# Moving the second half of group 2 and all of group 3 from VectorE to GpSimd in the step back from the FP6 grid

## What is computed

```python
h = _layernorm(x) * (1 + cb) + sb            # cb, sb, gb: per batch
blocks = h.reshape(rows, K // 32, 32)
scales = max(max(abs(blocks)) / 7.5, eps)    # one per block of 32
xq = nearest_on_fp6_grid(blocks / scales)    # "to the grid"
xd = xq * scales                             # "from the grid"
out = xd @ wd.T + bias                       # 512 x 512 weights
x = x + gb * out
```

## Time and profile before

| what | us |
|---|---|
| median of 3 runs | 339.31 |
| lowest and highest | 336.63, 339.8 |
| profiled execution | 338.35 |
| span of its instructions | 336.3 |
| TensorE busy | 304.5 |
| VectorE busy | 290.4 |
| ScalarE busy | 239.9 |
| GpSimd busy | 227.5 |

### The profile page before, as it was taken

How to read it: one execution, slowest core, us unless ns; L and a number is a source line. 1 busy time by engine, 2 the same in 40 slices (tenths; PEclk the granted TensorE clock), 3 DMA queues, 4 the chain that set the end, 5 groups by cost and what they waited for, 6 DMA issues and landing times. The chain is left out here.

```text
span 336.3 us, 6060 instructions
## 1 busy us (share of the span) xinstructions
PE 304.5 (91%) x2159; PEld 227.8 (68%) x2159; DVE 290.4 (86%) x512; ACT 239.9 (71%) x536; POOL 227.5 (68%) x122
## 2 busy tenths in 40 slices
PE   7879999785899989998999999996999998998993
PEld 5213547565798777786888678874787785776782
DVE  4678759979999799799989979999798899989753
ACT  3278845698679979799998989976799875322410
POOL 1449393599748886969999996977878967722100
PEclk9999998979699999999999999999799999999999
DMA  6999699999979839996899699964773693303133
GB/s 185 394 406 399 231 150 239 355 307 346 225 174 241 154 134 225 276 212 232 136 236 271 221 229 247 248 175 79 228 117 127 185 146 142 127 0 125 49 140 94
DMA packets 23971, 69.00 MB, mean 205 GB/s; under 512 B 2387, under 2 KB 2516, under 8 KB 19974
## 3 DMA queue, kind: packets, MB, share of 16 engines
q1 hardware_dynamic: 16304, 53.83, 48.0%
q0 software_dynamic: 7392, 14.68, 26.0%
q10 hardware_dynamic: 246, 0.12, 0.2%
HBM read 51.48 MB, written 17.14 MB: 204 GB/s over the span
## 5 line engine op out<-in xcount | busy, mean ns | idle before, releaser
L746 PE MATMUL ps<-WH,XH 128*128 128x512 f32 x256 | 108.8, 427 | 1.1 <-issue 0.9
L746 PE MATMUL ps<-WL,XH 128*128 128x512 f32 x256 | 103.3, 405 | 0.0
L379 POOL TENSOR_TENSOR U<-U,c_bc 128x1024 f32<-128x1024 f32 x31 | 74.6, 2408 | 39.0 <-ACT U L474 38.4
L390 POOL TENSOR_TENSOR U<-U,sb_bc 128x1024 f32<-128x1024 f32 x31 | 74.4, 2399 | 2.5
L746 PE MATMUL ps<-WH,XL 128*128 128x512 f32 x256 | 69.7, 394 | 0.2 <-DVE XL L1196 0.2
L463 ACT COPY ps<-bias_bc 128x512 f32<-128x512 f32 x61 | 36.0, 590 | 38.9 <-DVE X L1261 38.9
L1255 DVE TENSOR_TENSOR ps<-ps,gb_bc 128x512 f32<-128x512 f32 x64 | 44.3, 692 | 15.7 <-PE ps L746 15.6
L746 PEld LDWEIGHTS ps<-WH,XH 128*128 128x128 f32 x256 | 50.0, 195 | 11.0 <-ACT XH L454 2.0
L746 PEld LDWEIGHTS ps<-WL,XH 128*128 128x128 f32 x256 | 50.2, 196 | 10.2 <-issue 1.1
L746 PEld LDWEIGHTS ps<-WH,XL 128*128 128x128 f32 x256 | 48.9, 191 | 11.8 <-DVE XL L1196 0.7
L454 ACT ACTIVATE XH<-ps 128x512 fp32r<-128x512 f32 x64 | 37.5, 587 | 22.8 <-PE ps L724 22.7
(11 more groups left out here) (212 smaller groups left out, 351.1 us busy)
## 6 DMA issues: line engine op xcount, KB each, us to landing
X<-in_x SPq DMA_DIRECT2D x16, 1024.0 KB, 8.6
out<-X SPq DMA_DIRECT2D x15, 1024.0 KB, 4.7
X<-mod_scratch POOLq DMA_DIRECT2D x14, 1024.0 KB, 10.9
X<-in_wmod SPq DMA_DIRECT2D x2, 1024.0 KB, 12.3
sb_bc<-mod_scratch SPq DMA_DIRECT2D x7, 256.0 KB, 8.0
c_bc<-mod_scratch SPq DMA_DIRECT2D x7, 256.0 KB, 6.6
gb_bc<-mod_scratch SPq DMA_DIRECT2D x7, 256.0 KB, 8.2
msp<-mod_scratch SPq DMA_DIRECT2D x8, 160.0 KB, 9.8
```

Source lines behind the costliest of these rows:

```text
L379: nc.gpsimd.tensor_tensor(a, a, spread(c_bc[:, b % 2, :]), ALU.mult).then_inc(u_done, 2 if g == 0 else 1)
L390: nc.gpsimd.tensor_tensor(a, a, spread(sb_bc[:, b % 2, :]), ALU.add).then_inc(h_done, 2 if g == 0 else 1)
L746: return M(bank, a[:, k * P:(k + 1) * P], w[:, k, :], start=False, stop=last, skip_group_check=n >= 3)
```

## The change

The border between the engines moves from a whole group to a half. BY_VECTOR = 5 halves stay with VectorE, counted 2g+h: both halves of groups 0 and 1, and the first half of group 2. The halves (2, 1), (3, 0) and (3, 1) go to GpSimd, at the places in its list where later groups have them. VectorE copies the scales to s32 half by half for these three; from group 4 on still a group at a time. to_grid no longer waits for the copy's signal s32_done; GpSimd's from_grid does. Because GpSimd now reads Q8 for these halves, to_grid(3, 1) and to_grid(4, h) wait for xd1_done.

```diff
+        BY_VECTOR = 2 * 2 + 1
@@ GpSimd
             def from_grid(g, h):
                 pool.wait_ge(xt_done, TILES * (g - 2) + HALF * (h + 1))
+                pool.wait_ge(s32_done, 2 * g + h + 1 - BY_VECTOR)
                 pool.wait_ge(q_done, 2 * g + h + 1)
...
-                if g - 1 > FILLING:
+                if 2 * (g - 1) >= BY_VECTOR:
                     from_grid(g - 1, 0)
                 plus_sb(g, 1)
-                if g - 1 > FILLING:
+                if 2 * (g - 1) + 1 >= BY_VECTOR:
                     from_grid(g - 1, 1)
@@ TensorE, transposes
-                if g <= FILLING:
-                    pe.wait_ge(xd_done, 2 * g + j // HALF + 1)
+                half = 2 * g + j // HALF
+                if half < BY_VECTOR:
+                    pe.wait_ge(xd_done, half + 1)
                 else:
-                    pe.wait_ge(xd1_done, 2 * (g - FILLING - 1) + j // HALF + 1)
+                    pe.wait_ge(xd1_done, half - BY_VECTOR + 1)
@@ VectorE, block_scales
-                if g > FILLING:
-                    if g - 2 > FILLING:
-                        dve.wait_ge(xd1_done, 2 * (g - 2 - FILLING))
-                    W_.tensor_copy(s32[:, g % 2, :, :], s64).then_inc(s32_done, 1)
+                if 2 * g + h0 >= BY_VECTOR:
+                    if 2 * (g - 2) + h1 > BY_VECTOR:
+                        dve.wait_ge(xd1_done, 2 * (g - 2) + h1 - BY_VECTOR)
+                    W_.tensor_copy(s32[:, g % 2, h0:h1, :], s64[:, h0:h1, :]).then_inc(s32_done, h1 - h0)
@@ VectorE, to_grid
-                if g > FILLING:
-                    dve.wait_ge(s32_done, g - FILLING)
-                    if g - 1 > FILLING:
-                        dve.wait_ge(xd1_done, 2 * (g - 2 - FILLING) + h + 1)
+                if 2 * (g - 1) + h >= BY_VECTOR:
+                    dve.wait_ge(xd1_done, 2 * (g - 1) + h + 1 - BY_VECTOR)
@@ VectorE, slots THIRD and SECOND
-                    from_grid(g, 1)
+                    if 2 * g + 1 < BY_VECTOR:
+                        from_grid(g, 1)
...
-                    from_grid(g, 0)
+                    if 2 * g < BY_VECTOR:
+                        from_grid(g, 0)
```

## The result

| | before | changed |
|---|---|---|
| median, us (10 runs each) | 338.79 | 335.45 |
| lowest and highest | 336.63, 339.83 | 333.47, 336.71 |
| profiled execution | 338.35 | 336.71 |
| its span | 336.3 | 334.9 |

The ratio is 0.9907 (95% interval 0.9887 to 0.9927): the change makes the kernel 0.9% or some 3.2 us faster. I had forecast 339.0 us with a range of 336.3 to 341.5, and 0.3 us of effect. That was wrong. In experiments 5, 9, 10 and 12 one or two single runs are over 1.5% slower than the fastest of their kernel: the medians given count them, the ratios and intervals leave them out, and the traces of experiments 5 and 9 are of such runs.

The account below looks back on a forecast made before the run. It took the path as VectorE's half (2, 0) until 85 us, TensorE until 106.8, ScalarE until 118, then TensorE; 338.35 - 0 - 0.3 = 338.05, on the median 339.31 - 0.3 = 339.0 us, range 336.3 to 341.5.

Parts of the forecast that it names:

- Value on the path: 0: Before 107 us: net 3.0 us taken off VectorE brings 0, bounds 0 and 3.7 us.
- The replay of GpSimd's list: 92 to 111 us: three added multiplications, 5.75 us, fit; delay taken in by GpSimd's idle 3.74 us before 128.98.
- the two transfers: Groups 6 and 7: issued 5.3 and 3.8 us later, landing before ScalarE's reads at 110.37 and, at median, 124.02.
- there the whole gain has turned into a longer wait: At 112.82 us VectorE, relieved earlier, waits for ScalarE; that wait was to be 1.4 us or longer.
- Rival A: VectorE leads from 85 to 110 us: 333.9 us at most, 336.3 with the first part alone; chance 0.05.
- Rival B: At 226 us L1134 escapes its collision with GpSimd's multiplication: 1.9 us less, 337.1 us; chance 0.08.
- The wait that to_grid loses: All 12 later groups: to_grid starts 0.1 to 0.2 us earlier each; bounds 0 to 2.4 us, 0.3 taken.
- in the chain that ended last there is one such place: At 212.31 us, the one place on that chain where VectorE leads and to_grid's earlier start counts: 0.2 us.
- The rule on two SBUF inputs: 92 to 111 us: relocated GpSimd work slows only VectorE instructions with two SBUF inputs; none in the three windows checked.

Follow-up runs that it names:

- experiment 5: Changed kernel with the one-column comparison near 226 us written as an operation with a scalar instead of two tensors: 333.04 us, ratio to before 0.9827.
- experiment 9: Changed kernel with the scalar form of experiment 5 and the head's five row casts and differences moved to VectorE's slot 1: 327.82 us, ratio to before 0.9672.
- experiment 10: Kernel of experiment 9 with the border as before the change (BY_VECTOR = 8, VectorE takes all of groups 2 and 3): 330.03 us, ratio to before 0.9734.
- experiment 12: The kernel of experiment 10 run once more, unchanged: 330.22 us, ratio to before 0.9724.
- experiment 2: Changed kernel with only the halves moved: GpSimd's wait for s32_done taken out, VectorE's put back: 338.58 us, ratio to before 1.0001.
- experiment 1: Changed kernel with the border put back (BY_VECTOR = 8), so only the waits are exchanged: 335.96 us, ratio to before 0.9920.
- experiment 4: Changed kernel without GpSimd's s32_done wait for the second half of every group from 4 on: 337.98 us, ratio to before 0.9973.
- experiment 6: Changed kernel with the head's five row casts and differences moved from VectorE's slots 5 and 6 to slot 7: 343.11 us, ratio to before 1.0133.

## Why the prediction was wrong

**The move itself: right.** "Value on the path: 0" is experiment 2, 1.0001. The replay of GpSimd's list came within 0.5 us at all three multiplications and the two transfers stayed in time. That the relief turns into waiting for ScalarE was right, the place wasn't: "there the whole gain has turned into a longer wait" names 112.82, where it should have been 102 and 106 us, and the wait at 113 us is 1.56 us in experiment 1 too, where nothing was relieved. Rival A, which came nearest to the measured time, was right in the number and wrong in the cause: with A, experiment 2 would have gained 3 us. Rival B didn't come: in the changed kernel the comparison of one column starts at 225.44, 0.26 us into GpSimd's multiplication, and still takes 2.14 us.

**The wait that to_grid loses: right in kind, too small.** The term was 0.3 us, with the one place of the chain at 212 us. By the trace of experiment 4 it is 0.4 to 0.6 us, and 0.9 by its ratio (0.1 to 1.7 by the interval). The mistake is in "in the chain that ended last there is one such place": that chain began only at 212.2 us and listed 9% of the span for VectorE; a stretch that it doesn't show isn't a stretch where VectorE never leads. The additions come 0.17 us earlier at tiles 15, 19, 35, 39, 43, 47 and 51, and 0.52 us at tile 23, much of which is given back one or two tiles later.

**The wait that GpSimd gets: the step that failed.** The prediction counts s32_done as a wait that "to_grid loses" and puts at nothing, without a reason, that from_grid gains it. The signal has always come by then, but the wait's cost on GpSimd is some 30 ns. Near 303 us these 30 ns decide which engine stands back, and that is 1.75 us on the path: more than half of the result. Why 30 ns suffice is not shown; I take it that with them VectorE reaches SBUF first. The trace of the kernel before held all that was needed: L1179 stands on the chain and in the order of time with 2.50 us, beside L1180 with 0.75 for the same shape but only one tensor in SBUF, and GpSimd's L366 starts 30 ns behind it. The rule on two SBUF inputs was weighed, but only in the 20 us where work moved ("of which VectorE's list has none in 92 to 94, 104 to 106 and 108 to 111 us"), and rival B applied it to one place of two. The new wait touches all 24 of GpSimd's multiplications from the grid, so all of them should have been looked at.

**What stays open.** The two terms, 1.75 us and 0.4 to 0.6, make 2.1 to 2.4 us of some 3.2 (2.5 to 3.8 by the interval). No run shows where the rest lies.

**The clock and the median.** Each profiled execution carries 1 to 2 us of its own (at tile 41 or between tiles 7 and 12). Had I read the result from the first profile alone, the terms would have been 0.7 us gained by tile 12 and 1.7 lost at tile 41. The same kernel profiled again loses 0.4 and 0.1 there. Both go with the granted clock: from 85 to 110 us it was 0.93 in the first profile, 0.90 before and 0.87 in the second.

## What to carry to other kernels

When a change moves a wait from one engine to another, list every instruction that now starts a little later or earlier, over the whole run, and look at each for an instruction of the neighbour that it may collide with; here 30 ns brought 1.75 us. An instruction that takes three times as long as another of its shape is to be suspected of a collision, and it is worth more attention than a full engine: here two edits to such instructions brought 2.4%, while moving 3.7 us of work off a busy VectorE brought nothing. Before free time on an engine is filled with work, look at what its neighbour does in it.

## What the runs showed of the hardware

Where VectorE's instruction with two SBUF inputs starts 30 to 40 ns ahead of GpSimd's by the rows, it is still the one that stands back (2.50 us, GpSimd 1.91 unchanged; before and experiments 2 and 4); with 60 to 70 ns it goes first (0.76) and GpSimd takes 2.46, in the other eleven traces. One more wait on a signal that has come costs GpSimd some 30 ns (0.17 us behind the releasing instruction, was 0.14). Casts from SBUF to SBUF take 0.41 to 0.48 us alone (experiment 9) and 2.45 to 2.93 beside GpSimd (experiment 6), though they have a single input. The step to the grid that waits for its own engine's copy starts 0.20 to 0.22 us behind the reciprocal ahead of the copy (0.55 once); without the wait it starts 0.03 us behind, overlapping the copy.
